# Every second attention step of a gated cross-attention block gets its probabilities transposed by VectorE and a way through DRAM

## The reference, cut to what matters

```
h   = rmsnorm(layernorm(x))                       # x: 8 batches x 128 tokens x 512
q, k, v = h @ w_q.T, ctx @ w_k.T, ctx @ w_v.T     # 32 heads of 128
score = q k^T + position_bias[head];  score = where(mask, score, -inf)
P     = where(mask, softmax(score), 0)
attn  = P v;   out = attn @ w_out.T + residual
x = x + tanh(g_xattn) * out
x = x + tanh(g_ffn) * (base linear + top-2 LoRA experts of layernorm(x))
```

## The kernel before, in words

| j | ACT before the exps | ACT after the exps | DVE after `scores(s+1)` |
|---|---|---|---|
| 0 | copy, split, copy, copy, split | nothing | weight sum, `wq_lo`, `wq_lo`, Q sum |
| 1 | split, copy | copy, split | K sum, `wq_lo`, `wq_lo`, weight sum |
| 2 | copy, copy, split | split | `wq_lo`, Q sum, K sum, `wq_lo`, weight sum |
| 3 | split | copy | Q sum, K sum, `wq_lo`, weight sum |

## Time and profile before

### The profile page before, as it was taken

The page is one execution under the profiler, slowest core; times in us unless marked ns, Lnnn a source line. Parts: engine busy times, 40 slices in busy tenths (PEclk is TensorE's granted clock), DMA queues, the critical chain, the costliest instruction groups (busy, mean ns, idle before and its releaser), DMA issues.

```text
span 817.2 us, 13043 instructions
## 1 busy us (share of the span) xinstructions
PE 810.3 (99%) x4286; PEld 689.3 (84%) x4286; DVE 638.7 (78%) x997; ACT 497.1 (61%) x1164; POOL 294.5 (36%) x309
## 2 busy tenths in 40 slices
PE   9999999999999999999999999999999999999998
PEld 7787887888888888888888888888888788888886
DVE  6976476557887898688888888977887976789875
ACT  4646655447666666766666666667677677666311
POOL 1113230002456365455555563564733600003230
PEclk9999999999999999999999999999999999999999
DMA  9565455688545665565575466655598999997011
GB/s 324 157 194 169 118 165 168 218 247 257 168 146 190 189 199 161 193 212 149 180 220 173 147 192 187 189 172 193 173 308 308 367 387 386 328 325 263 20 46 59
DMA packets 132594, 168.52 MB, mean 206 GB/s; under 512 B 9392, under 2 KB 84016, under 8 KB 132272
## 3 DMA queue, kind: packets, MB, share of 16 engines
q1 hardware_dynamic: 132528, 167.70, 63.0%
HBM read 111.04 MB, written 62.91 MB: 213 GB/s over the span
## 4 chain that ended last, share of the span: by engine, by line
PE 90%; DVE 7%; issue 1%; ACT 1%; POOL 1%; DMA 1%; DVEq 0%; SPq 0%; POOLq 0%
PE bank L328 71%; PE bank L1514 7%; PE bank L1531 7%; PE bank L1522 3%; DVE t_hl L1014 1%; DVE s_hl L1014 1%; DVE stats L1018 1%; DVE wv L1014 1%; DMA raw_v<-in_w_v 1%; PE bank L1620 0%; PE bank L1457 0%; DVE stage L1075 0%; DVE acc L1250 0%; POOL xs L598 0%; DVE cb L1014 0%
## 5 line engine op out<-in xcount | busy, mean ns | idle before, releaser
L328 PE MATMUL bank<-cb,wq 128*128 128x512 f32 x672 | 177.2, 399 | 0.0
L328 PE MATMUL bank<-xb,wq 128*128 128x512 f32 x672 | 177.2, 399 | 0.0
L328 PE MATMUL bank<-t_hl,s_hl 128*128 128x512 f32 x672 | 158.0, 393 | 0.1
L328 PE MATMUL bank<-wv,cb 128*128 128x512 f32 x672 | 154.7, 391 | 1.5 <-DVE wv L1014 1.1
L328 PEld LDWEIGHTS bank<-wv,cb 128*128 128x128 f32 x672 | 125.6, 188 | 29.6 <-DVE wv L1014 3.0
L328 PEld LDWEIGHTS bank<-t_hl,s_hl 128*128 128x128 f32 x672 | 124.6, 188 | 26.2 <-DVE s_hl L1014 0.6
L654 POOL TENSOR_TENSOR bm<-bias_sb,mneg 128x512 f32<-128x512 f32 x64 | 74.6, 1166 | 197.4 <-DVE pr L1180 161.5
L328 PEld LDWEIGHTS bank<-cb,wq 128*128 128x128 f32 x672 | 121.9, 189 | 22.8
L328 PEld LDWEIGHTS bank<-xb,wq 128*128 128x128 f32 x672 | 121.8, 189 | 22.7
L860 ACT ACTIVATE pr<-pr,nmax 128x128 f32<-128x128 f32 x256 | 99.3, 394 | 7.2 <-DVE nmax L1182 7.2
L1014 DVE TENSOR_TENSOR t_hl<-t_raw,t_hl 128x1024 fp32r<-128x1024 f32 x56 | 72.1, 1287 | 21.0 <-ACT t_hl L871 20.8
(11 more groups left out here) (158 smaller groups left out, 1169.9 us busy)
## 6 DMA issues: line engine op xcount, KB each, us to landing
t_raw<-t_spill SPq DMA_DIRECT2D x56, 512.0 KB, 5.5
v_spill<-stage SPq DMA_DIRECT2D x64, 256.0 KB, 3.1
raw<-in_w_qk SPq DMA_DIRECT2D x32, 512.0 KB, 5.8
v_sb<-v_spill SPq DMA_DIRECT2D x64, 256.0 KB, 3.1
s_raw<-s_spill SPq DMA_DIRECT2D x56, 256.0 KB, 5.6
t_spill<-x_at SPq DMA_DIRECT2D x48, 256.0 KB, 3.3
s_piece<-in_w_o SPq DMA_DIRECT2D x64, 128.0 KB, 3.5
s_spill<-s_piece SPq DMA_DIRECT2D x32, 256.0 KB, 3.6
```

Of the source, the lines that this page charges most:

```text
L328: mm = pe.matmul(dst, a, b, start=first and n == 0, stop=last and n == total - 1, skip_group_check=True)
```

## The change

With `TURN_EVERY = 2`, odd steps (`by_quads(s)`) no longer use PE's transposes. ACT scales the probabilities by `rinv` in PSUM (`scale_rows`), DVE transposes the tile in 32x32 blocks (`turn`, into `turned`), SP stores `turned` to DRAM with four DMAs of 64 KB (`store_turned`) and loads it back as one 256 KB tile in the right order (`load_pt`, into `pt`). In even steps ACT scales from PSUM into `turned`, PE transposes `turned` back into the same PSUM bank, and ACT copies that into `pt`. The scores now stay in two PSUM banks that alternate (`pr` is a pair of banks, `ps_s` and `ps_t` are gone); bias add, maximum and exps work there. DVE's multiply by `rinv` is gone from both kinds of steps. `attention` and all that follows from it (`copy_attention`, `store_at`, `T_SUMS`) come one step later. PE reads `pt` in four runs of 32 columns.

```diff
+TURN_EVERY = 2
-            pt_sb = sb("pt_sb", [P, W], on=second)
-            pr = sb("pr", [P, 2, W], on=second)
+            turned = sb("turned", [P, W], on=second)
+            pt = sb("pt", [P, 2, W], on=second)
-        ps_s, ps_t, ps_at = bank[1], bank[2], bank[3]
+        pr, ps_at = [bank[1], bank[2]], bank[3]
+            def store_turned(s):
+                sp.wait_ge(turned_ok, turns(s) + 1)
+                for i in range(QUADS):
+                    sp.dma_start(p_dram[turns(s) % 2, :, i, :].rearrange("(j c) n -> c j n", j=QUADS),
+                                 turned[QUAD * i:QUAD * i + QUAD, :].rearrange("c (j n) -> c j n", j=QUADS)).then_inc(turned_stored, 16)
+            def load_pt(s):
+                sp.wait_ge(turned_stored, 16 * QUADS * (turns(s) + 1))
+                if s >= 2:
+                    sp.wait_ge(a_ps, s - 1)
+                sp.dma_start(pt[:, s % 2, :], p_dram[turns(s) % 2, :, :, :].rearrange("p i n -> p (i n)")).then_inc(pt_in[s % 2], 16)
...
+            def scale_rows(s):
+                act.wait_ge(inv_ok, 2 * s + 2)
+                into = pr[s % 2]
+                if not by_quads(s):
+                    into = turned
+                    if s:
+                        act.wait_ge(turned_stored, 16 * QUADS * (turns(s - 1) + 1))
+                for k in range(HALF):
+                    last = act.activation(into[:, cols(k)], pr[s % 2][:, cols(k)], ACT.Copy, scale=rinv[:, k:k + 1])
+                last.then_inc(pr_ok, 1)
...
-                    copy_attention(s - 1)
+                    scale_rows(s)
+                    copy_attention(s - 2)
...
-                    act.activation(pt_sb[:, :], ps_t[:, :], ACT.Copy).then_inc(pt_ok, 1)
+                    if not by_quads(s):
+                        act.wait_ge(t_ps, turns(s) + 1)
+                        act.activation(pt[:, s % 2, :].rearrange("p (i k q) -> p k i q", i=QUADS, k=HALF),
+                                       pr[s % 2][:, :].rearrange("p (k i q) -> p k i q", k=HALF, i=QUADS), ACT.Copy).then_inc(pt_ok, 1)
...
-                ve.wait_ge(inv_ok, 2 * s + 2)
-                own = pr[:, s % 2, :].rearrange("p (b k) -> p b k", b=HALF)
-                ve.tensor_tensor(own, own, rinv[:, :].unsqueeze(2).to_broadcast([P, HALF, P]), ALU.mult).then_inc(pr_ok, 1)
+            def turn(s):
+                ve.wait_ge(pr_ok, s + 1)
+                ve.wait_ge(t_ps, turns(s) + 1)
+                if turns(s):
+                    ve.wait_ge(turned_stored, 16 * QUADS * turns(s))
+                ve.transpose(turned[:, :].rearrange("p (j k n) -> p j k n", j=QUADS, k=HALF),
+                             pr[s % 2][:, :].rearrange("p (k j n) -> p j k n", k=HALF, j=QUADS)).then_inc(turned_ok, 1)
...
+                    if by_quads(s):
+                        turn(s)
                     if s + 1 < STEPS:
                         scores(s + 1)
...
-                    transposes(s)
+                    if not by_quads(s):
+                        transposes(s)
...
-                    attention(s)
+                    if s:
+                        attention(s - 1)
```

More of the change, by code:

```diff
@@ L308, in cols, with by_quads, turns, pt_batch @@
             return slice(P * k, P * k + P)
+        def by_quads(s):
+            return s % TURN_EVERY == TURN_EVERY - 1
+        def turns(s):
+            return s // TURN_EVERY
+        def pt_batch(s, k):
+            return pt[:, s % 2, :].rearrange("p (i k q) -> p k i q", i=QUADS, k=HALF)[:, k, :, :]
         def v_evac(g, m, t):
@@ L522, in _ @@
             for p in range(PAIRS):
-                if p + 2 < PAIRS:
-                    sp.wait_ge(wq_lo_ok, NP * (p + 1))
-                    load_wq(p + 2)
                 for j in range(4):
                     s = 4 * p + j
-                    store_at(s)
-                    if s + VRING < STEPS:
-                        sp.wait_ge(a_ps, s + 1)
-                        load_v(s + VRING)
-                    store_sums(s)
-                    if s % 2 == 0 and s + 2 < STEPS:
+                    if by_quads(s):
+                        store_turned(s)
+                    if j == 0 and p + 2 < PAIRS:
+                        sp.wait_ge(wq_lo_ok, NP * (p + 1))
+                        load_wq(p + 2)
+                    if s % 2 and s + 1 < STEPS:
                         store_piece(s // 2)
-                    elif s % 2 and s + 1 < STEPS:
-                        load_piece((s + 1) // 2)
                     if j == 2 and p + 2 < PAIRS:
@@ L539, in _ @@
                         load_bias(p + 2)
+                    if by_quads(s):
+                        load_pt(s)
+                    store_sums(s)
+                    if s:
+                        store_at(s - 1)
+                        if s - 1 + VRING < STEPS:
+                            sp.wait_ge(a_ps, s)
+                            load_v(s - 1 + VRING)
+                    if s % 2 and s + 1 < STEPS:
+                        load_piece((s + 1) // 2)
                     for n in EARLY_LOADS.get((p, j), ()):
@@ L545, in _ @@
                 load_o(n)
-                if n < FIRST_LOAD + 3:
+                if n < FIRST_LOAD + LATE_SUMS:
+                    if n == FIRST_LOAD + LATE_SUMS - 2:
+                        store_at(STEPS - 1)
                     store_sums(STEPS + n - FIRST_LOAD)
@@ L706, in _ @@
             s_sums(STEPS // 2 - 1)
-            for s in range(STEPS, STEPS + 3):
+            for s in range(STEPS, STEPS + LATE_SUMS):
                 t_sums(s)
@@ L859, in softmax_exp @@
                 for k in range(HALF):
-                    last = act.activation(pr[:, s % 2, cols(k)], pr[:, s % 2, cols(k)], ACT.Exp, bias=nmax[:, k:k + 1],
+                    last = act.activation(pr[s % 2][:, cols(k)], pr[s % 2][:, cols(k)], ACT.Exp, bias=nmax[:, k:k + 1],
                                           accum_out=sums[:, k:k + 1])
                 last.then_inc(exp_ok, 1)
+            def scale_rows(s):
[8 more added lines that the diff above has]
+                last.then_inc(pr_ok, 1)
             def o_hi(n):
@@ L923, in _ @@
                         o_hi(n)
-            copy_attention(STEPS - 1)
+            copy_attention(STEPS - 2)
             def tokens1_hi(t):
@@ L1187, in probabilities @@
                 ve.wait_ge(exp_ok, s + 1)
+                if s:
+                    ve.wait_ge(pr_ok, s)
                 ve.reciprocal(rinv[:, :], sums[:, :]).then_inc(inv_ok, 1)
@@ L1510, in scores @@
                     pe.wait_ge(ed_ok, 6 * p + 2 * j + 2)
-                if s:
-                    pe.wait_ge(scored, s)
+                if s >= 2:
+                    if by_quads(s):
+                        pe.wait_ge(turned_ok, turns(s - 2) + 1)
+                    else:
+                        pe.wait_ge(pt_ok, turns(s - 2) + 1)
                 for k in range(HALF):
-                    last = pe.matmul(ps_s[:, cols(k)], q_sb[:, j, cols(k)], k_sb[:, j, cols(k)], start=True, stop=True)
+                    last = pe.matmul(pr[s % 2][:, cols(k)], q_sb[:, j, cols(k)], k_sb[:, j, cols(k)], start=True, stop=True)
                 last.then_inc(s_ps, 1)
             def transposes(s):
-                if s:
-                    pe.wait_ge(pt_ok, s)
                 pe.wait_ge(pr_ok, s + 1)
                 for k in range(HALF):
-                    last = pe.transpose(ps_t[:, cols(k)], pr[:, s % 2, cols(k)], ident[:, :])
+                    last = pe.transpose(pr[s % 2][:, cols(k)], turned[:, cols(k)], ident[:, :])
                 last.then_inc(t_ps, 1)
             def attention(s):
-                pe.wait_ge(pt_ok, s + 1)
+                if by_quads(s):
+                    pe.wait_ge(pt_in[s % 2], 16 * (turns(s) + 1))
+                else:
+                    pe.wait_ge(pt_ok, turns(s) + 1)
                 pe.wait_ge(v_in[s % VRING], 16 * (s // VRING) + 16)
@@ L1530, in attention @@
                 for k in range(HALF):
-                    last = pe.matmul(ps_at[:, cols(k)], v_sb[:, s % VRING, k, :], pt_sb[:, cols(k)], start=True, stop=True)
+                    last = pe.matmul(ps_at[:, cols(k)].rearrange("p (i q) -> p i q", i=QUADS), v_sb[:, s % VRING, k, :],
+                                     pt_batch(s, k), start=True, stop=True)
                 last.then_inc(a_ps, 1)
@@ L1644, in _ @@
                 output(n)
+                if n == LAST_ATTENTION:
+                    attention(STEPS - 1)
             out_transposes(0)
```

29 lines of the change are left out of this document (18 added, 11 removed).

## The result

The changed kernel takes 843.75 us (median of 6 runs, 838.85 to 845.12) against 819.90 beside it: 1.0273 times as long, interval 1.0256 to 1.0291. The forecast was 832.1 us, in a range of 807 to 851. The direction was right and the size was half of what came. The profiled run took 839.67 us, with a span of 837.9 (+20.7); the runs above 843 us show lower mean granted clocks (0.985 to 0.989, against 0.994 in the profiled run), so the rest of the 23.9 goes with the clock.

What follows compares the result with a forecast made beforehand. The prediction took PE to bound the kernel, busy for all of the loop, and the loop between ACT and DVE to set the end after the change: 820.06 + 12.0 = 832.1 us, in a range of 807 to 851.

Steps and rivals of the forecast that it cites:

- PE's gain: Attention loop: without odd steps' transposes PE saves 0.45 us per odd slot, 0.90 per pair, and alone needs 27.25.
- The loop between ACT and DVE: Attention loop: ACT and DVE wait in turn, 28.95 us per pair; costs 0.80 per pair, 12.0 over 15 pairs.
- The signs asked for: Loop: PE's L1589 waits for L915, about 1 us in even slots; L915 waits for L1248, L1256 for L915.
- signs of being wrong: PE without waits at 27.25 per pair; ACT or PE waiting for DMA on turned or pt; L1601 groups above 0.89.
- The bounds of 27.25 and 30.2: Loop per pair: low with cheaper exps and scalings in PSUM and no POOL disturbance, high with a transpose of 1.24 us.
- the prediction's 0.48 and 0.69 for sixteen: Possible savings per pair on exps in PSUM: 0.48 us at 0.03 each, or 0.69 by the skill's 43 ns.
- The prediction's estimate of 1.24 us for VectorE's transpose: DVE's transpose in odd slots: high end 1.24 us, from the skill's 311 ns four times; 0.62 was taken.
- As long as the stores land in time: SP's odd slot: four stores and a load, 0.43 us of issue each, cost nothing on this condition.
- The rival: DRAM way decides: even-step scaling waits for odd stores, binding from landing L of 3.4 us; within 0.10 for above 851.
- In pair 15 I take no change: Last pair: no weights left to split, but output splits stand in their place, so no change in cost.
- The last attention and its stores lie in the output stage, about 2 us: End of the kernel: the later attention costs about 2 us, cancelled by a lag of about 2 at the start.
- The runs of 32 columns in PE's reading of `pt`: Attention on PE: reading pt in runs of 32 columns costs nothing, range 0 to a doubled 0.89 us per attention.

Runs made afterwards that it cites:

- dve_mult_last8: Against both: multiply by rinv back on DVE, even steps into pt, no turn in the last eight steps; 810.88 us, ratio 0.9887.
- two_tiles: Against the changed kernel: even steps scaled into their own slot of pt instead of the shared turned; 832.34 us, ratio 1.0141.
- best: Against the changed kernel: even steps into pt, DVE's multiply, turn up to step 53, attention in its own step from 55 on; 807.74 us, ratio 0.9841.
- dve_shared: Against dve_mult_last8: even steps multiplied into the one shared tile turned instead of pt; 811.33 us, ratio 0.9887.
- both: Against the changed kernel: even steps scaled into pt, and no turn in the last eight steps; 821.99 us, ratio 1.0032.
- lag_end: Against both: turn only up to step 53, attention in its own step from 55 on, two attentions in step 55 (catch-up); 818.71 us, ratio 0.9981.
- pe_last8: Against the changed kernel: no turn in the last eight steps, PE transposes odd steps there; 830.62 us, ratio 1.0123.
- stores_ahead: Against two_tiles: in the last two pairs SP issues an even slot's output loads behind the next odd slot's stores; 827.55 us, ratio 1.0079.

## Why the prediction was right about the sign and wrong about the size

**PE's gain: right.** 0.90 per pair and 27.25 for PE alone; measured 0.95 and 27.20 (dve_mult_last8).

**The loop between ACT and DVE: right mechanism, too dear.** The signs asked for are there: PE's L1589 waits for L915 (22.1 us in 25 waits of its weight loads up to 577 us, 0.9 each; "about 1 us in even slots"), ACT's L915 for L1248, DVE's L1256 for L915. Taking the loop away brings pairs to 27.20 with the shared tile or without it, so it is the cause of the loss in the body of the loop. One of the signs of being wrong came as well: ACT waits for DMA on `turned`, 27.3 us up to 577 us. But the prediction had the loop at 28.95 per pair, while with the stores out of the way it is 27.74 (two_tiles). The terms that were mis-sized, to be read beside the earlier trace rows: the changed kernel's timelines of ACT and of DVE, a group of DVE's lines there (190 to 588 us), and the other weight sum in two_tiles (190 to 570 us).

```profile
422.69 1.12 ACT L915 ACTIVATE bank<-bank,rinv 128x128 f32<-128x128 f32 x4 [0.44 <-DVE rinv L1248]
423.70 0.62 ACT L952 ACTIVATE g_at<-bank 128x512 f32<-128x512 f32 x1
...
425.90 0.34 ACT L902 ACTIVATE bank<-bank,nmax 128x128 f32<-128x128 f32 x1 [0.58 <-DVE nmax L1238]
...
426.26 0.33 ACT L902 ACTIVATE bank<-bank,nmax 128x128 f32<-128x128 f32 x1
...
427.29 0.61 ACT L888 ACTIVATE tmp<-bank 128x512 f32<-128x512 f32 x1
```

```profile
423.83 0.72 DVE L1256 STREAM_TRANSPOSE turned<-bank 128x512 f32<-128x512 f32 x1 [1.18 <-ACT bank L915]
424.48 0.67 DVE L1236 TENSOR_TENSOR bank<-bank,bm 128x512 f32<-128x512 f32 x1
```

```profile
L1196 DVE TENSOR_TENSOR sq<-sq,raw 128x512 f32<-128x512 f32 x14 | 10.1, 722 | 0.0
```

```profile
L1200 DVE TENSOR_TENSOR sq<-raw 128x512 f32<-128x512 f32 x13 | 12.1, 932 | 0.0
```

Four exps in PSUM take 1.39 to the next instruction (425.90 to 427.29), not 1.54: 0.15 less at j = 1 and at j = 2. (At j = 0 DVE waits for the last accumulator read, and nothing is saved.) The scaling is 0.10 cheaper in each of four slots: ACT's next instruction starts 1.01 after the first of the four (422.69 to 423.70), and the transpose starts 1.14 after it, crossing included. The weight sums, which were priced by their means beside a busy POOL, are 0.22 less (L1196, 0.722) and 0.29 less (L1200, 0.932). The transpose is 0.65 from start to start where 0.62 was taken, two times. That is 28.95 - 0.30 - 0.40 - 0.51 + 0.06 = 27.80, beside 27.74 measured. With L1200 as in the changed kernel (0.758) it would be 27.63, so the fit is good to about 0.2: within that the sum was sound, and its prices came from rows that lay too far away. The bounds of 27.25 and 30.2 held it. One slip: the sum holds twelve exps, since those of j = 3 are not in it, so the prediction's 0.48 and 0.69 for sixteen were a third too large.

The Trainium skill's figure (VectorE: DVE Perf Modes, The TRN2 errata) that ScalarE pays 52 cycles less with PSUM as the source, an estimate of 43 ns, is borne out in size: an exp's median was 393 ns from SBUF to SBUF and is 347 from PSUM to PSUM. The prediction's estimate of 1.24 us for VectorE's transpose, four times the 311 ns that the Trainium skill gives for 128x128 of 2-byte data (the same page, The three transpose paths), did not hold: 128x512 of 4-byte data takes 0.717 us (x32, 706 to 720 ns). By the runs, the advice of the Trainium skill to leave 128x128 to TensorE (the same page, Rules for kernel authors) depends on who waits: best is faster with 27 tiles turned by VectorE.

**"As long as the stores land in time": the step that failed.** The rival had the right place (the even step's scaling into `turned`) and the right formula. L counts there from 3.91 us after `rinv`, so the 7.9 and 6.2 us after which the changed kernel's stores are seen landed make it 4.0 at j = 1 and 2.3 at j = 3, one over the bound of 3.4 and one under it; 3.5 had been taken for a store four times as large, and the quarters held to be sooner. It adds 0.68 per pair there (28.42 against 27.74), and only on top of the loop between ACT and DVE: with DVE's multiply it adds nothing (dve_shared).

**"In pair 15 I take no change": the largest miss.** It is 6.8 us from step 58 to step 63 and about half of the 10.0 behind it (an end of 203.6 in two_tiles, 199.1 in both). The stores' median from issue to landing is 2.6 us up to 588 us and 5.5 from 588 to 660 us, and they stand behind the output loads in SP's list. The earlier trace rows already had the sign: the same kind of store took 5.0 instead of 3.5 in that stretch.

**"The last attention and its stores lie in the output stage, about 2 us": mis-sized.** It is 4.2 to 5.2 us in four kernels with no turn in the last eight steps (ends of 198.1 to 199.1, against 193.8 in the kernel before and in lag_end; the fifth, pe_last8, has 200.7, and what it has more was not traced), since SP waits for POOL's last sum with all output loads behind it. The prediction counted the work that came later, and not what stands behind it in SP's list.

**The runs of 32 columns in PE's reading of `pt`: right at nothing.** Attention groups take 0.89 from start to start (435.09 to 435.98), as before.

So the forecast had 12.0 us in 15 pairs and nothing elsewhere; the 20.7 us of the profiled span came as 3.8 up to step 58 and 16.8 in the last five steps and the handover. Two errors partly cancelled: the loop was too dear by 8, the end too cheap by 17. That the time fell inside the range is luck in part: its upper end, 851, stood for a slow transpose or for late stores in every pair, and neither is what came.

**What stays open.** Why the stores land 1.4 to 3.6 us after the last issue at j = 1 (3.4 at 443.88 to 447.24) and only 1.4 to 2.2 at j = 3 (dve_shared, steps 5 to 55) was not separated from the traffic around them: 1 MB of weights is issued some 6 us ahead of the former, in slot j = 0. The 3.7 us around the catch-up in lag_end, 1.4 in best (50.9 against 49.5), were not traced further. How much of the 843.75 is lowered clock was read from the granted clock alone; no run varied it.

## What to carry to other kernels

Ask of a moved instruction not how long it takes but which engine's answer it waits for: here the same scaling cost about 0.6 us of DVE's time for each step and no time in the pair, while on ACT it closed a ring between two engines that were busy for three quarters of the time. A transfer is hidden or not by what stands between its start and the first write that must wait for it, slot by slot, so price it where the queue is fullest and behind what it is queued, not at its median. And a step that is made later by one is paid where the loop ends, with everything queued behind its store.

## What the runs showed of the hardware

VectorE's transpose of 128x512 four-byte elements in 32x32 blocks, out of PSUM into SBUF, takes 0.717 us, about as long as an add of the same size (0.683), and not a multiple of it. ACT's scaled copy of 128 columns takes 0.342 us from PSUM to PSUM and 0.369 from PSUM to SBUF. A store of 64 KB of 512-byte pieces lands in 2.6 us (median of the changed kernel) beside the loop's traffic and in 5.5 beside the output loads; there the last of four was seen landed 6.9 us after its issue in stores_ahead. PE's waits of 3.48 and 3.64 us were followed by a lower granted clock, 0.86 over the windows of 12 us that hold them; no window of the kernel before's loop shows that.
